# A routed FFN block: gathered rows transposed by the DMA engines in place of TensorE

## The chip, the cores and the metric

One core of a Trainium2 chip runs the kernel. The metric is device time in microseconds (us) of one execution; the time before the change is the median of three runs.

## The reference

`x` is (4, 512, 512), 2,048 tokens of 512 features. A first part adds to it a 512 x 512 matrix per batch, made from scores of a context, of which each row keeps its largest 153. The second part, in which the change lies, is a mixture of experts on the normalised tokens:

```python
logits = x @ router_w.T
topk_w, topk_idx = jax.lax.top_k(softmax(logits), 2)      # 2 of 8 experts a token
topk_w = topk_w / jnp.sum(topk_w, axis=-1, keepdims=True)
...
out = jax.nn.silu(x @ gw) * (x @ uw) @ dw                 # 512 -> 352 -> 512, for each expert
return (acc + ce[:, None] * out, None)
...
shared = jax.nn.silu(x @ s_gate_w + s_gate_b) * (x @ s_up_w + s_up_b) @ s_down_w + s_down_b   # 512 -> 704 -> 512
return (moe_out + shared)
```

## The kernel before

The kernel computes in float16 pairs: a value is a high half plus a low half, and a product is three matmuls (high x high, high x low, low x high). `xn_dram` holds for each token 1,024 float16, the 512 high halves and then the 512 low halves of its normalised row.

**Stages.** Four batches go through attention, residual, normalisation and the shared expert. The last batch's shared expert overlaps with the routing: VectorE and TensorE sort the 4,096 (token, expert) pairs into blocks of 128 that have one expert each. There are at most 39 blocks (`BLOCKS`); with these inputs 35 are run. `run_blocks` (L1443) writes the first 21 out, loops over the next 12 two at a time and takes the rest behind a test of how many are in use.

**One routed block**, number j, parity p = j mod 2:

- GpSimd, `gather` (L538): copies a column of indices to `gidx` (L539) and starts an indirect DMA (L540) of 128 rows of `xn_dram` into `xg[p]`, which lies in `qT` or `kT`, 256 KB.
- TensorE, `routed_x` (L1001): eight float16 transposes (L1009) of `xg[p]` into PSUM bank 0. VectorE, `routed_x` (L1396), copies the bank to `xT2` (L1401), where a parity has one buffer.
- TensorE, `routed_up` (L1012): 24 matmuls of 352 columns (L1023 to L1028), with `xT2` as stationary operand and the expert's gate and up weights moving. Where they lie comes from `where(j)`, a register load from `wbase`.
- ScalarE, `routed_sig` (L785): the Silu of the gate. VectorE, `routed_hidden` (L1407): times the up part.
- TensorE, `routed_hT` (L1031): three float32 transposes (L1036) of the hidden rows to bank 1. ScalarE, `routed_h` (L791), writes the high half and VectorE, `routed_h` (L1412), the low half.
- TensorE, `routed_down` (L1039): nine matmuls of 512 columns (L1047 to L1049).
- ScalarE, `routed_y` (L799): times the token's weight, into `y2[p]`, when the scatter that last used the buffer (j - 2) has landed.
- GpSimd, `scatter` (L543): waits for `y2` and for the landing of the scatter before (tokens can be in both), copies the indices to `sidx` (L551) and starts an indirect DMA (L552) that adds the 128 rows to the output in DRAM.

**Order on each engine**, fixed by `step(j)`. TensorE: hidden transposes of j-1, eight row transposes of j+1, up of j, down of j-1. ScalarE: `routed_h(j-1)`, in the first 21 blocks two conversions of weights (`split_hi`, L600), `routed_sig(j)`, `routed_y(j-1)`. VectorE: `routed_h(j-1)`, `routed_x(j+1)`, in the first 21 blocks two `weight_lo` (L1101), `routed_hidden(j)`. GpSimd: gather(j+3), which waits until the rows of block j+1 have been transposed out of the same buffer, then scatter(j-1). SyncE loads weights through four staging places (L396), each again when VectorE or GpSimd is done with it; the last loads are issued about 480 us into the span.

**Start.** GpSimd gathers blocks 0 and 1, adds three tiles of the shared output, waits for block 0's transposes, gathers block 2 and adds the fourth tile. TensorE transposes the rows of block 0 ahead of the last shared down projection. ScalarE writes four shared outputs (`shared_out`, L693) with weight conversions between them.

Of the kernel before, what the change touches and what calls it, by code (L numbers as in the profile page):

```python
# [5 lines left out]
F32 = mybir.dt.float32  # L6
F16 = mybir.dt.float16
# [6 lines left out]
P = 128  # L14
NB, S, D = 4, 512, 512
# [4 lines left out]
KD = D // P  # L20
# [25 lines left out]
DC, SC = len(DOWN_ROWS), len(SH_ROWS)  # L46
# [9 lines left out]
BLOCKS = T * TOPK // P + E - 1  # L56
# [38 lines left out]
SECOND_AT = [2, 2, 2, 1]  # L95
# [27 lines left out]
def build(nc, x, ctx_in, wq, wk, gamma, router, gate, up, down, s_gate, s_gate_b, s_up, s_up_b, s_down, s_down_b,  # L123
# [3 lines left out]
    def sb(name, shape, dt=F32):  # L127
        return es.enter_context(nc.sbuf_tensor(name, shape, dt))

    def sem(name):  # L130
        return es.enter_context(nc.semaphore(name))
# [22 lines left out]
    xT = sb("xT", [P, 2, KD, S], F16)  # L154
# [6 lines left out]
    ident16 = sb("ident16", [P, P], F16)  # L161
# [37 lines left out]
    xg = [t[:, :].bitcast(F16) for t in (qT, kT)]  # L199
# [3 lines left out]
    y2 = xb[:, 0:2, :]  # L203
    h2 = xb[:, 2:4, 0:I]
    sg2 = sgt[:, :, 0:I]
    xT2 = xT[:, :, :, :].rearrange("p s c t -> p (s c t)")[:, 0:4 * KD * P].rearrange("p (a s c t) -> p a s c t", a=2, s=2, c=KD)
    hT2 = hS[:, :, 0:DC, 0:2 * P].rearrange("p s c (a t) -> p s c a t", a=2)
    rt = sigA[:, :, :].rearrange("p a b -> p (a b)")
# [51 lines left out]
    bank = [es.enter_context(nc.psum_tensor(f"bank{i}", [P, 512], F32)) for i in range(8)]  # L260
# [10 lines left out]
    d_y = [sem(f"d_y{i}") for i in range(2)]  # L271
    d_stage = [sem(f"d_stage{i}") for i in range(PLACES)]
    d_xg = [sem(f"d_xg{i}") for i in range(2)]
    d_sc = [sem(f"d_sc{i}") for i in range(2)]
    s_const = sem("s_const")
    s_zero = sem("s_zero")
# [26 lines left out]
    s_gu = sem("s_gu")  # L303
# [20 lines left out]
    s_oneh = sem("s_oneh")  # L324
    s_tabp = sem("s_tabp")
    s_route = sem("s_route")
    s_x2ps = sem("s_x2ps")
    s_x2 = sem("s_x2")
    s_gu2 = sem("s_gu2")
    s_sig2 = sem("s_sig2")  # L330
    s_h2 = sem("s_h2")
# [6 lines left out]
    s_held = sem("s_held")  # L338
# [100 lines left out]
    def _(pool):  # L439
# [44 lines left out]
        def add_shared(b, t, src):  # L484
            g = TB * b + t
            pool.wait_ge(s_y, g + 1)
            pool.wait_ge(d_x1, 16 * TB * (b + 1))
            pool.dma_start(out[g * P:(g + 1) * P, :], src, accum_op=ALU.add).then_inc(d_y[t % 2], 16)
# [77 lines left out]
        gather(1, 1)  # L566
        for t in range(TB - 1):
            add_shared(NB - 1, t, ylasts[t])
        pool.wait_ge(s_x2ps, 1)
        gather(2, 0)  # L570
        add_shared(NB - 1, TB - 1, ylasts[TB - 1])

        def step(j, m, p, fetch=True):
            if fetch:
                pool.wait_ge(s_x2ps, j + 2)
                gather(j + 3, 1 - p)
            if not (isinstance(j, int) and j == 0):
                scatter(j - 1, m if p else m - 1, 1 - p)
# [10 lines left out]
    def _(act):  # L589
# [12 lines left out]
        def split_some(k):  # L602
            for _ in range(k):
                split_hi(next(loads))
# [88 lines left out]
        def shared_out(b, t, dst):  # L693
            g = TB * b + t
            act.wait_ge(s_yps, g + 1)
            if b < NB - 1 and g >= 2:
                act.wait_ge(d_y[t % 2], 16 * (g // 2))
            act.activation(dst, bank[4 + t][:, :], ACT.Copy, scale=1.0 / HW).then_inc(s_y, 1)
# [75 lines left out]
        act.wait_ge(s_xnT, NT)  # L774
        for i in range(2):
            act.wait_ge(d_xn[i], 16 * NT // 2)
        for t in range(TB):
            shared_out(NB - 1, t, ylasts[t])
            if t == 0:
                split_some(FIRST_AT[SC])  # L780
            split_some(SECOND_AT[t])

        def routed_sig(j, p):
            act.wait_ge(s_gu2, j + 1)
            act.activation(sg2[:, p, :], bank[4 + 2 * p][:, 0:I], ACT.Silu, scale=1.0 / XW).then_inc(s_sig2, 1)  # L785
# [7 lines left out]
        def routed_y(j, m, p):  # L793
            act.wait_ge(s_y2ps, j + 1)
            if isinstance(j, int) and j < 2:
                act.wait_ge(d_y[p], 16 * NT // 2)
            else:
                act.wait_ge(d_sc[p], 16 * m)
            act.activation(y2[:, p, :], bank[2 + p][:, :], ACT.Copy, scale=wcol[:, bass.ds(j, 1)]).then_inc(s_y2, 1)  # L799

        def step(j, m, p, fetch=True):
            first_block = isinstance(j, int) and j == 0
            if not first_block:
                routed_h(j - 1, 1 - p)
            if isinstance(j, int) and j < HEAD_BLOCKS:
                split_some(BLOCK_UNITS)
            routed_sig(j, p)
            if not first_block:
                routed_y(j - 1, m if p else m - 1, 1 - p)

# [2 lines left out]
        def finish(j):  # L813
            routed_h(j, j % 2)
            routed_y(j, j // 2, j % 2)

        run_blocks(act, used, step, finish)

    @block.tensor
    def _(pe):  # L820
# [177 lines left out]
        shared_down(NB - 1, 1)  # L998
        shared_down(NB - 1, 2)

        def routed_x(j, m, p):  # L1001
            pe.wait_ge(d_xg[p], 16 * (m + 1))
            if isinstance(j, int) and j == 0:
                pe.wait_ge(s_route, 1)
            else:
                pe.wait_ge(s_x2, j)
            o = bank[0][:, :].bitcast(F16)
            for c in range(2 * KD):
                last = pe.transpose(o[:, c * P:(c + 1) * P], xg[p][:, c * P:(c + 1) * P], ident16[:, :])  # L1009
            last.then_inc(s_x2ps, 1)  # L1010

        def routed_up(j, p, at):  # L1012
            pe.wait_ge(s_x2, j + 1)
            if not (isinstance(j, int) and j < 2):
                pe.wait_ge(s_h2, j - 1)
            else:
                pe.wait_ge(s_y, NT - 2 + 2 * j)
            og, ou = bank[4 + 2 * p][:, 0:I], bank[5 + 2 * p][:, 0:I]
            for c in range(KD):
                hi, lo = at + (GU_HI + c * GU), at + (GU_LO + c * GU)  # L1020
                xh, xl = xT2[:, p, 0, c, :], xT2[:, p, 1, c, :]
                f, z = c == 0, c == KD - 1
                pe.matmul(og, xh, W[:, bass.ds(hi, I)], start=f, stop=False)  # L1023
                pe.matmul(ou, xh, W[:, bass.ds(hi + I, I)], start=f, stop=False)  # L1024
                pe.matmul(og, xh, W[:, bass.ds(lo, I)], start=False, stop=False)  # L1025
                pe.matmul(ou, xh, W[:, bass.ds(lo + I, I)], start=False, stop=False)  # L1026
                pe.matmul(og, xl, W[:, bass.ds(hi, I)], start=False, stop=z)  # L1027
                last = pe.matmul(ou, xl, W[:, bass.ds(hi + I, I)], start=False, stop=z)  # L1028
            last.then_inc(s_gu2, 1)
# [25 lines left out]
        def step(j, m, p, fetch=True):  # L1055
            first_block = isinstance(j, int) and j == 0
            if not first_block:
                routed_hT(j - 1, 1 - p)
            if first_block or not (isinstance(j, int) and j == BLOCKS - 1):
                routed_x(j + 1, m + (1 if p else 0), 1 - p)  # L1060
            at = where(j)
            if not isinstance(j, int):
                pe.wait_ge(s_wloD, EARLY + (E - 1) * PER_EXPERT)
            elif j == 0:
                pe.wait_ge(s_wlo, SECOND - EARLY)
            elif j % 4 == 0 and j < HEAD_BLOCKS:
                pe.wait_ge(s_wloD, EARLY + j // 4 * PER_EXPERT)
            routed_up(j, p, at)
            if not first_block:
                routed_down(j - 1, 1 - p, where(j - 1))  # L1070

        routed_x(0, 0, 0)
        shared_down(NB - 1, TB - 1)

        def finish(j):
# [6 lines left out]
    def _(dve):  # L1082
# [243 lines left out]
        for k in range(2):  # L1326
            last = dve.tensor_tensor(sel[:, k, :, :], ef[:, k, :].rearrange("p (g o) -> p g o", o=1).to_broadcast([P, NT, E]),
                                     io8.rearrange("p (o e) -> p o e", o=1).to_broadcast([P, NT, E]), ALU.is_equal)
# [20 lines left out]
        for k in range(2):  # L1349
            last = dve.tensor_tensor(prod[:, k, :, :], sel[:, k, :, :], slotr, ALU.mult)  # L1350
# [42 lines left out]
        dve.tensor_scalar(wcol[:, :], tab[:, 1, :], 1.0 / HW, None, ALU.mult)  # L1393
        dve.scalar_tensor_tensor(idx[:, :], tab[:, 0, :], -1.0, zer, ALU.add, ALU.add).then_inc(s_route, 1)

        def routed_x(j, p):  # L1396

            dve.wait_ge(s_x2ps, j + 1)
            if not (isinstance(j, int) and j < 2):
                dve.wait_ge(s_gu2, j - 1)  # L1400
            dve.tensor_copy(xT2[:, p, :, :, :].rearrange("p s c t -> p (s c t)").bitcast(F32), bank[0][:, :]).then_inc(s_x2, 1)  # L1401

        def routed_hidden(j, p):
            dve.wait_ge(s_sig2, j + 1)
            if not (isinstance(j, int) and j < 2):
# [9 lines left out]
        def step(j, m, p, fetch=True):  # L1415
            first_block = isinstance(j, int) and j == 0
            if not first_block:
                routed_h(j - 1, 1 - p)
            if first_block or not (isinstance(j, int) and j == BLOCKS - 1):
                routed_x(j + 1, 1 - p)  # L1420
            if isinstance(j, int) and j < HEAD_BLOCKS:
                later_weights(BLOCK_UNITS)
            routed_hidden(j, p)
# [3 lines left out]
        def later_weights(k):  # L1427
            for _ in range(k):
                weight_lo(next(later))

        later_weights(4)
        routed_x(0, 0)
        later_weights(sum(SECOND_AT) - 4)

        def finish(j):
            routed_h(j, j % 2)
# [51 lines left out]
```

## Time and profile before

| | us |
|---|---|
| median of three runs | 600.37 (599.4 to 602.25) |
| the profiled execution | 601.87 |
| its span in the profile | 599.7 |
| TensorE busy (PE) | 489.7, 82% |
| VectorE busy (DVE) | 355.1, 59% |
| ScalarE busy (ACT) | 241.0, 40% |
| GpSimd busy (POOL) | 194.9, 32% |
| mean granted TensorE clock | 0.908 of full speed |

The span runs from the first to the last recorded instruction of one execution; the execution's own time has some two microseconds around it. PE is TensorE's matmuls, PEld its weight loads, DVE is VectorE, ACT ScalarE, POOL GpSimd and SPq SyncE's queue of DMA issues. A matmul's busy time includes its pipeline, so that TensorE can look busy while it could take more. "idle before" names what the engine was last waiting for.

### The profile page before, as it was taken

The page shows a single profiled execution, that of the slowest core. Times are in us where ns is not written, and L with a number is a line of the kernel's source. Part 1 is how long each engine was busy: PE and PEld are TensorE (multiplying, and loading weights), DVE is VectorE, ACT ScalarE, POOL GpSimd, SP SyncE. Part 2 cuts the span into 40 slices and gives each one's busy share as a digit, 9 for nine tenths or more (in the row PEclk, how much of TensorE's full clock was granted, in tenths as well). Part 3 has the DMA queues.
Part 4 walks back from the last instruction along what each step waited for, and adds up shares of the span by engine and source line. Part 5 has one row for each costly group of instructions (what it writes and reads, how often), then busy time and mean ns, then how long its engine had stood idle before and what let it go on. Part 6 is the DMA issues. An engine that isn't in the chain of part 4 may idle for free.

```text
span 599.7 us, 9826 instructions
## 1 busy us (share of the span) xinstructions
PE 489.7 (82%) x2994; PEld 273.9 (46%) x2995; DVE 355.1 (59%) x987; ACT 241.0 (40%) x433; POOL 194.9 (32%) x245
## 2 busy tenths in 40 slices
PE   6120439959899598968899999999999999999970
PEld 2000324414444154434445555666666666666640
DVE  2799787688586886878269745454554542322210
ACT  4643265353735337451634243443534432222220
POOL 1031243001500033000606743445445454454531
PEclk9565769979899699997999999999999999999985
DMA  6601240003710037001622386777887745445451
GB/s 173 205 18 35 89 147 12 1 1 84 196 21 1 1 107 176 0 0 72 135 79 66 109 230 169 205 178 179 175 200 189 169 87 87 89 80 95 71 91 17
DMA packets 36415, 60.51 MB, mean 101 GB/s; under 512 B 5641, under 2 KB 16137, under 8 KB 36370
## 3 DMA queue, kind: packets, MB, share of 16 engines
q0 software_dynamic: 10384, 23.34, 22.6%
q1 hardware_dynamic: 25986, 36.60, 19.3%
q8 instruction: 25, 0.41, 0.3%
q14 instruction: 20, 0.16, 0.1%
HBM read 37.64 MB, written 22.28 MB: 100 GB/s over the span
## 4 chain that ended last, share of the span: by engine, by line
PE 66%; DVE 20%; issue 5%; ACT 5%; POOL 2%; DMA 1%; DVEq 0%; SPq 0%; POOLq 0%; ACTq 0%
PE bank L912 5%; PE bank L913 5%; PE bank L914 5%; PE bank L1047 4%; PE bank L1049 4%; PE bank L1048 4%; PE bank L1023 3%; PE bank L1025 3%; PE bank L1026 3%; PE bank L1028 3%; PE bank L1027 3%; PE bank L1024 3%; PE bank L927 3%; PE bank L1009 3%; PE bank L929 3%
## 5 line engine op out<-in xcount | busy, mean ns | idle before, releaser
L912 PE MATMUL bank<-xT,W 128*128 128x512 f16 x192 | 74.0, 385 | 0.0
L913 PE MATMUL bank<-xT,W 128*128 128x512 f16 x192 | 73.9, 385 | 0.0
L914 PE MATMUL bank<-xT,W 128*128 128x512 f16 x192 | 73.8, 384 | 0.0
L552 POOL DMA_INDIRECT out_dram<-xb,sidx x35 | 57.0, 1627 | 30.1 <-POOL sidx L551 27.8
L1412 DVE TENSOR_TENSOR hS<-bank,hS 128x384 f16<-128x384 f32 x35 | 19.5, 558 | 73.7 <-ACT hS L791 69.6
L785 ACT ACTIVATE sgt<-bank 128x352 f32<-128x352 f32 x35 | 16.2, 463 | 86.6 <-PE bank L1028 86.6
L1407 DVE SCALAR_TENSOR_TENSOR xb<-bank,sgt 128x352 f32<-128x352 f32 x35 | 18.3, 524 | 54.0 <-ACT sgt L785 53.4
L799 ACT ACTIVATE xb<-bank,wcol 128x512 f32<-128x512 f32 x35 | 24.0, 687 | 56.8 <-PE bank L1049 52.3
L482 POOL TENSOR_TENSOR rstd<-pw 128x4 f32<-128x4 f32 x12 | 13.0, 1087 | 103.7 <-DVE pw L1129 103.7
L1023 PE MATMUL bank<-W,xT 128*128 x140 | 43.8, 313 | 0.6 <-issue 0.5
L1025 PE MATMUL bank<-W,xT 128*128 x140 | 43.8, 313 | 0.0
L1024 PE MATMUL bank<-W,xT 128*128 x140 | 43.8, 313 | 0.0
L1026 PE MATMUL bank<-W,xT 128*128 x140 | 43.8, 313 | 0.0
L1027 PE MATMUL bank<-W,xT 128*128 x140 | 43.8, 313 | 0.0
L1028 PE MATMUL bank<-W,xT 128*128 x140 | 43.8, 312 | 0.0
L652 ACT ACTIVATE sgt<-bank,bias 128x512 f32<-128x512 f32 x24 | 16.5, 687 | 66.9 <-PE bank L914 66.9
L1047 PE MATMUL bank<-W,hS 128*128 x105 | 40.5, 386 | 1.3 <-DVE hS L1412 1.3
L1048 PE MATMUL bank<-W,hS 128*128 x105 | 40.6, 386 | 0.0
L1049 PE MATMUL bank<-W,hS 128*128 x105 | 40.6, 386 | 0.0
L927 PE MATMUL bank<-W,hS 128*128 128x512 f16 x96 | 39.1, 407 | 0.0
L928 PE MATMUL bank<-W,hS 128*128 128x512 f16 x96 | 38.7, 403 | 0.0
L929 PE MATMUL bank<-W,hS 128*128 128x512 f16 x96 | 38.6, 402 | 0.0
(232 smaller groups left out, 1114.9 us busy)
## 6 DMA issues: line engine op xcount, KB each, us to landing
xn_dram<-xn SPq DMA_DIRECT2D x17, 256.0 KB, 2.4
xb<-x_in SPq DMA_DIRECT2D x4, 1024.0 KB, 6.4
out_dram<-xb SPq DMA_DIRECT2D x16, 256.0 KB, 2.1
out_dram<-ysh POOLq DMA_DIRECT2D x12, 256.0 KB, 5.1
stage<-L_ffn_down_w_in SPq DMA_DIRECT2D x12, 256.0 KB
sim<-L_ffn_down_w_in SPq DMA_DIRECT2D x12, 256.0 KB
stage<-L_ffn_gate_w_in SPq DMA_DIRECT2D x16, 176.0 KB
stage<-L_ffn_up_w_in SPq DMA_DIRECT2D x16, 176.0 KB
```

The lines of the kernel that those rows point to most:

```text
L912: pe.matmul(o, wh, xT[:, 0, c, :], start=(c == 0), stop=False)
L913: pe.matmul(o, wh, xT[:, 1, c, :], start=False, stop=False)
L914: last = pe.matmul(o, wl, xT[:, 0, c, :], start=False, stop=(c == KD - 1))
L1023: pe.matmul(og, xh, W[:, bass.ds(hi, I)], start=f, stop=False)
L1024: pe.matmul(ou, xh, W[:, bass.ds(hi + I, I)], start=f, stop=False)
L1025: pe.matmul(og, xh, W[:, bass.ds(lo, I)], start=False, stop=False)
L1026: pe.matmul(ou, xh, W[:, bass.ds(lo + I, I)], start=False, stop=False)
L1027: pe.matmul(og, xl, W[:, bass.ds(hi, I)], start=False, stop=z)
L1028: last = pe.matmul(ou, xl, W[:, bass.ds(hi + I, I)], start=False, stop=z)
L1047: pe.matmul(o, hh, wh, start=(c == 0), stop=False)
L1048: pe.matmul(o, hh, wl, start=False, stop=False)
L1049: last = pe.matmul(o, hl, wh, start=False, stop=(c == DC - 1))
```

## The change

The eight transposes of a block on TensorE, PSUM bank 0's part in them and VectorE's copy go. In their place ScalarE issues one transposing DMA a block (`dma_start_transpose`) from `xg[p]` in SBUF to `xT2[p]` in SBUF, 128 rows x 1,024 float16. It waits for the gather of its block. For blocks 0 and 1 it is issued among the last shared outputs, after the shared outputs of tiles 1 and 2 and the two weight conversions behind each; for block j+2 it is issued in ScalarE's `step(j)` between `routed_sig(j)` and `routed_y(j-1)`. `routed_up` waits on the DMA's semaphore. GpSimd's gathers wait on it too, where they waited for TensorE's transposes. The order of the other work is the same.

```diff
+    xt2 = xT[:, :, :, :].rearrange("p s c t -> p (s c t)")[:, 0:4 * KD * P].rearrange("p (a n t) -> p a n t", a=2, n=2 * KD)
...
+    d_xt = [sem(f"d_xt{i}") for i in range(2)]
...
-        pool.wait_ge(s_x2ps, 1)
+        pool.wait_ge(d_xt[0], 16)
         gather(2, 0)
...
             if fetch:
-                pool.wait_ge(s_x2ps, j + 2)
+                pool.wait_ge(d_xt[1 - p], 16 * (m + 1 + p))
                 gather(j + 3, 1 - p)
...
+        def routed_x(m, p):
+            act.wait_ge(d_xg[p], 16 * (m + 1))
+            act.sem_inc(s_held, 1)
+            act.dma_start_transpose(xt2[:, p, :, :], xg[p][:, :]).then_inc(d_xt[p], 16)
+
         for t in range(TB):
             shared_out(NB - 1, t, ylasts[t])
             if t == 0:
                 split_some(FIRST_AT[SC])
             split_some(SECOND_AT[t])
+            if t in (1, 2):
+                act.wait_ge(s_gu, NB * SC)
+                routed_x(0, t - 1)
...
             routed_sig(j, p)
+            if not (isinstance(j, int) and j + 2 >= BLOCKS):
+                routed_x(m + 1, p)
             if not first_block:
                 routed_y(j - 1, m if p else m - 1, 1 - p)
...
         def finish(j):
             routed_h(j, j % 2)
             routed_y(j, j // 2, j % 2)
+            for i in range(2):
+                act.wait_ge(d_xt[i], 16 * ((min(j + 2, BLOCKS - 1) + 2 - i) // 2))
...
-        def routed_x(j, m, p):
-            pe.wait_ge(d_xg[p], 16 * (m + 1))
+        def routed_up(j, m, p, at):
+            pe.wait_ge(d_xt[p], 16 * (m + 1))
             if isinstance(j, int) and j == 0:
                 pe.wait_ge(s_route, 1)
-            else:
-                pe.wait_ge(s_x2, j)
-            o = bank[0][:, :].bitcast(F16)
-            for c in range(2 * KD):
-                last = pe.transpose(o[:, c * P:(c + 1) * P], xg[p][:, c * P:(c + 1) * P], ident16[:, :])
-            last.then_inc(s_x2ps, 1)
-
-        def routed_up(j, p, at):
-            pe.wait_ge(s_x2, j + 1)
...
-            if first_block or not (isinstance(j, int) and j == BLOCKS - 1):
-                routed_x(j + 1, m + (1 if p else 0), 1 - p)
             at = where(j)
...
-        routed_x(0, 0, 0)
         shared_down(NB - 1, TB - 1)
...
-        def routed_x(j, p):
-
-            dve.wait_ge(s_x2ps, j + 1)
-            if not (isinstance(j, int) and j < 2):
-                dve.wait_ge(s_gu2, j - 1)
-            dve.tensor_copy(xT2[:, p, :, :, :].rearrange("p s c t -> p (s c t)").bitcast(F32), bank[0][:, :]).then_inc(s_x2, 1)
...
-        later_weights(4)
-        routed_x(0, 0)
-        later_weights(sum(SECOND_AT) - 4)
+        later_weights(sum(SECOND_AT))
```

## Rows read from the trace of the kernel before

**Rows 1.** The page's first line.

```profile
span 599.7 us, 9826 instructions
```

**Rows 2.** Stages, cut at scatters 0, 20 and 34 (x: instructions).

```profile
core 0: us, PE busy (x) PEld busy (x) DVE busy (x) ACT busy (x) POOL busy (x), PEclk, DMA share, GB/s
371.48:499.43 127.95, 127.95 (x896) 82.06 (x894) 63.81 (x111) 52.65 (x97) 63.24 (x80) 1.00 0.74 168
499.43:587.94 88.51, 82.75 (x552) 50.96 (x550) 21.24 (x38) 20.80 (x40) 40.73 (x55) 0.96 0.47 81
```

**Rows 3.** TensorE's timeline, one block, and a gap (start, duration, what).

```profile
444.93 0.49 PE L1036 MATMUL bank<-ident,xb 128*128 128x128 f32 x3
445.26 0.61 PE L1009 MATMUL bank<-ident,kT 128*128 128x128 f16 x8
445.70 0.31 PE L1023 MATMUL bank<-W,xT 128*128 x1
...
452.00 0.31 PE L1023 MATMUL bank<-W,xT 128*128 x1
...
503.01 0.32 PE L1023 MATMUL bank<-W,xT 128*128 x1 [0.48 <-issue]
```

**Rows 4.** GpSimd's timeline: scatters 3, 4, 9, 10, a cycle from scatter 21, scatter 25.

```profile
390.70 2.29 POOL L552 DMA_INDIRECT out_dram<-xb,sidx  x1 [0.84 <-POOL sidx L551]
...
399.09 1.61 POOL L552 DMA_INDIRECT out_dram<-xb,sidx  x1 [0.84 <-POOL sidx L551]
...
431.68 1.60 POOL L552 DMA_INDIRECT out_dram<-xb,sidx  x1 [0.84 <-POOL sidx L551]
...
437.59 1.61 POOL L552 DMA_INDIRECT out_dram<-xb,sidx  x1 [0.84 <-POOL sidx L551]
...
505.61 1.60 POOL L552 DMA_INDIRECT out_dram<-xb,sidx  x1 [0.84 <-POOL sidx L551]
506.65 0.77 POOL L539 COPY gidx<-idx 128x1 int32 x1
508.20 1.00 POOL L540 DMA_INDIRECT qT<-xn_dram,gidx  x1 [0.79 <-POOL gidx L539]
510.76 0.18 POOL L551 COPY sidx<-idx 128x1 int32 x1 [1.56 <-DMA out_dram<-xb,sidx]
511.80 1.61 POOL L552 DMA_INDIRECT out_dram<-xb,sidx  x1 [0.85 <-POOL sidx L551]
...
530.11 1.60 POOL L552 DMA_INDIRECT out_dram<-xb,sidx  x1 [0.84 <-POOL sidx L551]
```

**Rows 5.** GpSimd's waits, 371 to 531 us (total, times, longest).

```profile
POOL sidx L551 <- DMA out_dram<-xb,sidx: 38.6, 24, 3.0
...
POOL sidx L551 <- ACT xb L799: 0.9, 1, 0.9
```

**Rows 6.** Short stretches, columns as in rows 2.

```profile
396.00:398.00 2.00, 2.00 (x15) 1.30 (x14) 2.00 (x4) 0.86 (x2) 0.05 (x1) 1.00 0.94 328
...
574.00:575.00 1.00, 1.00 (x9) 0.64 (x8) 0.11 (x1) 0.00 (x0) 1.00 (x2) 1.00 0.00 0
```

**Rows 7.** Timeline of VectorE and TensorE where the routed stage starts.

```profile
359.99 0.61 DVE L1401 COPY xT<-bank 128x512 f32<-128x512 f32 x1
...
362.69 0.55 PE L1036 MATMUL bank<-ident,xb 128*128 128x128 f32 x3 [1.24 <-DVE xb L1407]
363.08 0.61 PE L1009 MATMUL bank<-ident,qT 128*128 128x128 f16 x8
```

**Rows 8.** SyncE's queue: one of its issues of a weight load.

```profile
391.69 0.34 SPq L396 DMA_DIRECT2D stage<-L_ffn_gate_w_in  x1
```

**Rows 9.** The page's DMA issues: count, KB each, us to landing.

```profile
out_dram<-xb SPq DMA_DIRECT2D x16, 256.0 KB, 2.1
...
kT<-ctx_in SPq DMA_DIRECT2D x4, 256.0 KB, 5.4
```

**Rows 10.** DMA queues, 400 to 480 us: packets, MB, share of 16 engines.

```profile
q0 software_dynamic: 2845, 6.61, 47.2%
q1 hardware_dynamic: 5505, 7.87, 33.3%
```

**Rows 11.** DMA queues, 500 to 530 us.

```profile
q0 software_dynamic: 1124, 2.63, 51.6%
```

**Rows 12.** Timeline of the last block: TensorE, and the last scatter.

```profile
580.32 0.52 PE L1036 MATMUL bank<-ident,xb 128*128 128x128 f32 x3 [2.21 <-issue]
...
582.10 0.60 PE L1047 MATMUL bank<-W,hS 128*128 x1 [1.26 <-DVE hS L1412]
582.50 0.63 PE L1048 MATMUL bank<-W,hS 128*128 x1
...
587.94 1.59 POOL L552 DMA_INDIRECT out_dram<-xb,sidx  x1 [0.85 <-POOL sidx L551]
```

More of the change, by code:

```diff
@@ L326, in build @@
     s_route = sem("s_route")
-    s_x2ps = sem("s_x2ps")
-    s_x2 = sem("s_x2")
     s_gu2 = sem("s_gu2")
@@ L1067, in step @@
                 pe.wait_ge(s_wloD, EARLY + j // 4 * PER_EXPERT)
-            routed_up(j, p, at)
+            routed_up(j, m, p, at)
             if not first_block:
                 routed_down(j - 1, 1 - p, where(j - 1))
-        routed_x(0, 0, 0)
         shared_down(NB - 1, TB - 1)
@@ L1418, in step @@
                 routed_h(j - 1, 1 - p)
-            if first_block or not (isinstance(j, int) and j == BLOCKS - 1):
-                routed_x(j + 1, 1 - p)
             if isinstance(j, int) and j < HEAD_BLOCKS:
```

## The prediction

> **What bounds the kernel now.** I read the stages first, then one block on TensorE, then GpSimd's queue, and last the DMA engines.
>
> The scatters of the routed stage run from 371.48 to 587.94 us of a span of 599.7 us [rows 1, 12]. The stage table is cut at scatters 0, 20 and 34: 127.95 us for 20 blocks with weight loads beside them (6.40 us a block), then 88.51 us for 14 blocks (6.32 us) without them. TensorE is busy in every microsecond of the first part [rows 2]. Its timeline shows the block's make-up: from one block's first up matmul (445.70) to the next one's (452.00) are 6.30 us, of which the three transposes of the hidden rows take 0.33 (444.93 to 445.26) and the eight transposes of the gathered rows 0.44 (445.26 to 445.70) [rows 3]. So TensorE looks like the bound, and the eight transposes a part of it.
>
> GpSimd's rows show a second chain that is as long. A scatter may start only when the one before has landed. In the cycle shown, the scatter starts at 505.61, the copy of the next indices starts at 510.76 once it has landed, 5.15 us later, and the next scatter at 511.80: 6.19 us [rows 4]. The gather lies in between and costs the chain nothing. From 371 to 531 us this engine waited 24 times for the scatter's landing before it could copy indices, against one wait for ScalarE in the same stretch [rows 5]. The cycle without loads is (530.11 - 505.61) / 4 = 6.12 us. With loads it is longer, once 8.39 us (390.70 to 399.09) [rows 4], where the DMA engines were 94% busy [rows 6]. That TensorE doesn't wait today is due to the two buffers of `y2`: from scatter 3 (390.70) to scatter 9 (431.68) pass 41.0 us against 6 x 6.30 on TensorE, so the scatters fall 3 us behind, and catch up later. Two bounds lie side by side then: TensorE at 6.30 us and the scatters at 6.12 us without loads, 6.40 us on average with them.
>
> **The change part by part.** One block costs this.
>
> TensorE loses 8 transposes, 0.44 us a block, and comes to 5.85 us. There are 36 such groups, so alone that would be 16 us. The register load of `where(j)` had them ahead of it; what stays ahead is down matmuls and the hidden rows' transposes, longer work than those, so I cost it at 0; if the cover is gone, the one gap of this kind is 0.48 us, before 503.01 [rows 3], and it would eat the whole saving.
>
> VectorE loses one PSUM copy a block (0.61 us for the one at 359.99 [rows 7]) and isn't on the path in the steady state: 63.81 us busy in 127.95 [rows 2].
>
> ScalarE gains one wait, for the gather of block j+2, and one DMA issue, both after `routed_sig(j)`. Queued behind them are `routed_y(j-1)`, `routed_h(j)` and two weight splits. The hold of the issue has no row: from below 0.33 us (an issue on SyncE's queue [rows 8]), from above 1.60 us (GpSimd's indirect one [rows 4]). I take 1.0, between the two. ScalarE is busy 52.65 us in 20 blocks [rows 2], 2.6 of 6.4 a block; of the 3.8 us left I count 2.5 as usable for a hold, since its pieces wait for other engines in between. The wait is harmless for the same reason: the gather starts at 508.20, right behind a scatter, so it has been on its way for most of a cycle by the time the next scatter starts, and what waits for ScalarE, the copy of the indices for `y2`, has some 3 us to spare once the scatters set the pace (a `y2` is written when the scatter before last has landed). `h(j)` is needed only when up(j+1) has run, 3.6 us after the hidden rows' transposes.
>
> The result's landing: 2.1 us for a plain 256 KB transfer at best, 5.4 at worst [rows 9]. It is needed two blocks less one up stage later, 2 x 5.85 - 3.6 = 8.1 us after up(j) ends. Hidden at both ends.
>
> GpSimd's gather(j+3) waits for the transposing DMA of j+1 in place of TensorE's transposes. That DMA is issued a block earlier, ahead of the `y2` of j-2 whose scatter GpSimd issues before this gather, so 0; behind the wait stands scatter(j-1), which a DMA of over about 5 us would begin to delay. SyncE's queue isn't touched.
>
> The 16 DMA engines get the work: 256 KB more a block. At the loads' rate (7.87 MB in 33.3% of 80 us, 3.4 us a MB) that is 0.89 us of all engines [rows 10]. Today they are busy 47.2 + 33.3% with loads, 5.2 of 6.40 us [rows 10], and 51.6% without, 3.2 of 6.12 us [rows 11]. So 2.9 us are free without loads and 1.2 with them. Bounds of what the scatter feels: 0 (all of it falls in the gap, as the empty microsecond after a gather shows [rows 6]) and 0.89 (all of it beside the scatter, as in the collision at 390 to 399 us, where the loads of two units, about 2 us, cost the cycle 2.3). On average the loads' 2.1 us a block cost the scatter 6.40 - 6.12 = 0.28, 13% of their time. With a gap of 1.2 us that share must grow; I take a quarter, 0.22 us, with loads, and 13%, 0.12 us, without.
>
> For the price in engine time the Trainium skill ("Advanced Engine Details and Errata", X-Bar Transpose) says that on trn2 transposing DMAs are as fast as regular ones. By that rule 0.89 stands. No run so far shows one.
>
> Start: the chain to block 1 runs through VectorE's copy at 359.99 and then the transposes of block 0's hidden rows at 362.69 and block 2's gathered rows behind them [rows 7]. Both copies go: 0.54 + 0.45 = -1.0 us. Block 0's and 1's transposing DMAs are issued behind shared outputs and land before 357 us, when the last shared matmul ends.
>
> End: the last block's tail (hidden rows at 580.32, down matmuls from 582.10 [rows 12], last scatter 587.94) takes 9.8 us from the end of the matmuls before it (580.32 - 2.21 = 578.11) and stays; TensorE is over 3 us ahead of the scatters by then, so scatter 34 follows scatter 33, not its tail.
>
> **The sum.** The profiled execution took 601.87 us (span 599.7 and 2.2 around it); the median of the runs is 1.5 lower. With TensorE at 5.85 the scatters set the pace throughout. Start -1.0; 20 blocks with loads x 0.22 = +4.4; 14 blocks x (6.12 + 0.12) = 87.4 against 88.5, -1.1. Together +2.3: 604.2, and 602.7 as a median. The expected 16 us are gone because the scatters, not TensorE, hold the stage.
>
> **The rivals.**
>
> Hidden: the DMA fits into the gaps. Start -1.0, loads 0, then 14 x 6.12 = 85.7 against 88.5, -2.8: -3.8, 596.6. For it: the engines' free time, and that the issue waits for the gather's landing, so it tends to fall right behind it. Against: only 1.2 us are free with loads.
>
> TensorE's saving shows in full: the scatters' cycle would have to close at 5.85, so 34 x 5.85 = 198.9 against 216.5, and -1.0: about 582. Against: the shortest cycle that I found is 5.91 us (431.68 to 437.59 [rows 4]), and the mean without loads 6.12.
>
> Slower, by contention: the transposing DMA's packets lie between the scatter's on the same engines, each block. It decides from 34 x d > 3.8 + 3, d = 0.2 us a scatter. With half of 0.89 (0.45): 20 x 0.45 + 14 x 6.57 - 88.5 - 1.0 = +11.5, 612; with all of it +26.5, 627. For it: 81% busy engines with loads, the collision row. Against: 13% so far.
>
> Much slower, by small pieces: if each row goes in pieces of 128 elements, 1,024 of them, at what a packet of the loads costs (5,505 in 33.3% of 80 us on 16 engines, 77 ns [rows 10]), that is 4.9 us of all engines a block: 10.1 in place of 6.40 with loads and 8.1 in place of 6.32 without, +74 + 25, about 700. For it: nothing in the trace. Against: shorter pieces should cost less than these 1.4 KB ones. Beside it stands a rule that speaks against the change: the Trainium skill ("VectorE: DVE Perf Modes", The three transpose paths) gives 1309 ns for a 128x128 transpose by DMA against 390 ns on TensorE; an estimate from that is 10.5 us for eight, if they go one by one, and the stage would take over 350 us. The row disagrees on TensorE already: eight take 0.44 us.
>
> **How the numbers follow.** About 0.5%, 3 us, is what a measurement can tell. The forecast (598 to 606) has 0.43, of it 0.33 within 0.5% and 0.10 above. Hidden 0.18 and TensorE in full 0.04 are faster, 0.22. Contention 0.25 and small pieces 0.10 are slower, with the forecast's upper part 0.45. The range 595.5 to 622 leaves out TensorE in full, small pieces and the worst of the contention.
>
> **What would show it.** Right: scatter starts 6.2 us apart after 500 us and 6.6 before, GpSimd's waits before the indices still on the DMA, TensorE with gaps before L1047 of some 0.3 us a block, full granted clock, scatter landing above 4.9 us where transposing packets lie beside it. Hidden: the same with 6.1. Small pieces: waits of ScalarE or TensorE on the transposing DMA itself, DMA share at 0.9 in all slices. Wrong altogether: scatter cycles under 6.0, or a granted clock that falls in the gaps as it does after the 2.2 us wait at the end, where a matmul takes 0.63 us [rows 12].

## The result and the profile after

The changed kernel takes 623.31 us (median of 4 runs, 620.64 to 625.85) against 600.85 us of the kernel before beside it: a ratio of 1.035 [1.031, 1.040]. It is slower by 3.5%. At the time first shown that is 600.37 x 1.035 = 621.5 us: just inside the range, far from the forecast's 602.7, and between the two ends of the contention rival, 612 and 627. The profiled execution took 620.64 us, with a span of 618.7. The ratios here and below leave out disturbed executions, of which one program, a_nosc, had two in four.

The stages, cut at scatters 0, 20 and 34 as in [rows 2]:

```profile
core 0: us, PE busy (x) PEld busy (x) DVE busy (x) ACT busy (x) POOL busy (x), PEclk, DMA share, GB/s
369.83:513.34 143.51, 125.72 (x736) 73.00 (x734) 51.27 (x90) 52.09 (x97) 63.05 (x80) 0.99 0.95 187
513.34:607.03 93.69, 78.13 (x448) 44.75 (x445) 13.37 (x25) 20.05 (x39) 40.83 (x54) 0.96 0.66 113
```

Three terms make the difference of the last scatter (607.03 against 587.94, +19.1): scatter 0 comes 1.65 us earlier, the 20 blocks with weight loads take 143.51 against 127.95 (+15.6), the other 14 take 93.69 against 88.51 (+5.2). TensorE, never idle before in the first part, is busy 125.72 of 143.51 us. The DMA engines' share is 0.95 where it was 0.74, and 0.66 where it was 0.47.

GpSimd's timeline, two cycles without loads (compare [rows 4]):

```profile
539.87 1.61 POOL L552 DMA_INDIRECT out_dram<-xb,sidx  x1 [0.85 <-POOL sidx L551]
...
545.66 0.19 POOL L551 COPY sidx<-idx 128x1 int32 x1 [2.19 <-DMA out_dram<-xb,sidx]
546.69 1.60 POOL L552 DMA_INDIRECT out_dram<-xb,sidx  x1 [0.84 <-POOL sidx L551]
...
553.29 1.61 POOL L552 DMA_INDIRECT out_dram<-xb,sidx  x1 [0.85 <-POOL sidx L551]
```

From a scatter's start to the copy that waits for its landing pass 5.79 us, 5.15 before. The cycle is 6.82 and 6.60 us here, and (600.99 - 513.34) / 13 = 6.74 on average up to scatter 33. GpSimd's and ScalarE's waits in the whole routed stage, and TensorE's gap in one block:

```profile
POOL sidx L551 <- DMA out_dram<-xb,sidx: 72.6, 34, 5.6
```

```profile
ACT xb L807 <- issue: 127.8, 29, 7.0
```

```profile
543.28 0.39 PE L1050 MATMUL bank<-W,hS 128*128 x1 [0.36 <-DVE hS L1405]
```

All 34 copies of indices behind the first scatter now wait for a scatter's landing; in the kernel before 25 copies did, and the other 10 waited for ScalarE. GpSimd waits for scatters to land, ScalarE's `routed_y` waits with it, and TensorE's gap before the down matmuls is where that shows. The profile names no releaser for ScalarE's wait, which is what its word "issue" says.

There is a second kind of wait. Who waited for the transposing DMAs themselves (total, times), and the longest of these waits, at the start:

```profile
  POOL gidx L539: 12.5, 6
  PE bank L1026: 7.7, 6
```

```profile
366.74 0.19 POOL L539 COPY gidx<-idx 128x1 int32<-128x1 int32 x1 [6.95 <-DMA xT<-qT]
```

GpSimd's gather waits for the landing six times and TensorE's up matmuls six times, all of it before scatter 20.

What the transposing DMAs themselves cost: the page's queue line, the queues from 520 to 560 us (6 transposing DMAs by their packets), the same from 400 to 480 us (11 of them; compare [rows 10, 11]), and how long an issue holds ScalarE's queue (least, median, most in ns):

```profile
q10 hardware_dynamic: 39072, 9.70, 10.7%
```

```profile
q0 software_dynamic: 1344, 3.15, 45.9%
q10 hardware_dynamic: 6336, 1.57, 20.7%
```

```profile
q0 software_dynamic: 2464, 5.77, 41.1%
q1 hardware_dynamic: 4785, 6.72, 32.3%
q10 hardware_dynamic: 11616, 2.88, 26.0%
```

```profile
L780 ACTq DMA_TRANSPOSE xT<-qT x19: 1247/1257/1576, 347.0 to 595.7; - x19
```

39,072 packets for 37 DMAs are 1,056 each, about 250 bytes. Without loads one DMA keeps all engines busy for 20.7% x 40 / 6 = 1.38 us, with loads for 26.0% x 80 / 11 = 1.89 us. The three queues with loads add up to 99.4%: there the engines are full. The hold on ScalarE's queue is 1.25 us.

Where these packets lie in a cycle, from the queues in short stretches of the cycle that starts with the scatter at 546.69 (the transposing DMA was issued at 546.63): 547.5 to 548.5, 548.5 to 549.0, 549.0 to 549.5, 549.5 to 550.5.

```profile
q10 hardware_dynamic: 539, 0.14, 69.7%
...
q10 hardware_dynamic: 341, 0.09, 101.6%
...
q0 software_dynamic: 16, 0.03, 95.0%
q10 hardware_dynamic: 176, 0.04, 37.0%
...
q0 software_dynamic: 44, 0.09, 86.7%
```

The transposing packets take most of the engines from 547.5 to 549 us, and the scatter's first packets appear only as they end, 2.5 us after its issue. The same reading in steps of 0.1 us gives 2.4 to 2.9 us for eight scatters from 519 to 567 us, against 1.9 to 2.2 us for six scatters of the kernel before. The coincidence is no chance: ScalarE issues the transposing DMA when the gather has landed, and the gather's packets lie right behind the scatter before, so that it comes out together with the next scatter. For the ten scatters from 526.56 to 587.43 us the two issues are at most 0.3 us apart.

### The profile page after: what moved, and what is told of

It is laid out like the page before. It is cut to its first block, busy times and chain, and to the rows that moved or that the text cites. A ratio compares the mean times of both kernels' runs of the same rounds, so it can differ in the third digit from the quotient of the medians.

```text
span 618.7 us, 9238 instructions
## 1 busy us (share of the span) xinstructions
PE 481.8 (78%) x2706; PEld 257.8 (42%) x2707; DVE 333.6 (54%) x951; ACT 239.7 (39%) x433; POOL 195.3 (32%) x245
## 3 DMA queue, kind: packets, MB, share of 16 engines
q1 hardware_dynamic: 25986, 36.60, 19.1%
q10 hardware_dynamic: 39072, 9.70, 10.7%
## 4 chain that ended last, share of the span: by engine, by line
DMA 34%; PE 29%; DVE 18%; issue 9%; ACT 4%; POOL 3%; POOLq 0%; DVEq 0%; SPq 0%; ACTq 0%
DMA out_dram<-xb,sidx 30%; PE bank L924 5%; PE bank L926 5%; PE bank L925 5%; PE bank L939 3%; PE bank L940 3%; PE bank L941 3%; PE bank L870 2%; DVE hS L1281 2%; DVE stats L1124 2%; DVE top L1203 1%; POOL sidx L551 1%; DVE sgt L1290 1%; DMA xT<-qT 1%; DVE W L1370 1%
## 5 line engine op out<-in xcount | busy, mean ns | idle before, releaser
L1050 PE MATMUL bank<-W,hS 128*128 x105 | 40.9, 390 | 14.6 <-DVE hS L1405 13.2
L1052 PE MATMUL bank<-W,hS 128*128 x105 | 41.1, 391 | 0.0
L1051 PE MATMUL bank<-W,hS 128*128 x105 | 41.0, 390 | 0.0
L684 ACT ACTIVATE signs<-sim,nprobe 128x512 int8<-128x512 f32 x40 | 28.4, 714 | 16.6 <-DVE probe L1167 8.6
L503 POOL PARTITION_ALL_REDUCE bad<-bad x4 | 1.5, 383 | 104.7 <-DVE bad L1188 104.7
```

## The experiments

Each is timed beside the kernel before on the same chip. Several leave out a part of the work; the expectation says which. "Cycle" is worked out from the starts of the scatters in each profile: with loads, scatter 0 to 20, divided by 20; without, scatter 20 to 33, divided by 13.

| kernel | us | ratio to before | cycle with loads | without |
|---|---|---|---|---|
| before | 600.9 to 602.9 | | 6.40 | 6.19 |
| changed | 623.3 | 1.035 [1.031, 1.040] | 7.18 | 6.74 |
| a_none | 593.1 | 0.987 [0.982, 0.992] | 6.31 | 5.98 |
| a_plain | 606.1 | 1.006 [1.003, 1.009] | 6.56 | 6.16 |
| a_half | 611.1 | 1.016 [1.011, 1.021] | 6.75 | 6.38 |
| b_extra | 627.7 | 1.046 [1.037, 1.055] | 7.18 | 6.81 |
| a_noload | 614.5 | 1.022 [1.018, 1.026] | 6.78 | 6.71 |
| b_early | 601.5 | 1.000 [0.998, 1.003] | 6.40 | 6.27 |
| a_early | 622.3 | 1.030 [1.021, 1.039] | 6.92 | 6.54 |
| a_move | 616.4 | 1.020 [1.016, 1.024] | 6.87 | 6.77 |
| a_move_early | 611.4 | 1.017 [1.012, 1.022] | 6.82 | 6.22 |
| a_none_early | 589.7 | 0.979 [0.976, 0.982] | 6.06 | 5.88 |
| b_nosc | 590.9 | 0.982 [0.977, 0.986] | | |
| a_nosc | 586.4 | 0.967 [0.959, 0.975] | | |

The theory that I began with was the rival of contention: the transposing packets delay the scatters, whose cycle bounds the stage. Its own rival was ScalarE's queue: in-order waits and the hold make `y2` late.

**a_none: the DMA away, the waits kept.**

```diff
-            act.dma_start_transpose(xt2[:, p, :, :], xg[p][:, :]).then_inc(d_xt[p], 16)
+            act.sem_inc(d_xt[p], 16)
```

> The changed kernel without the transposing DMAs: ScalarE still waits for the gather at the same places and TensorE multiplies whatever lies in xT2 (the routed part of the output is not computed from its rows). Contention theory (the transposing packets share the DMA engines with the scatter): scatter cycle back to 6.1 us without loads and 6.3 to 6.4 with them, against 6.7 and 7.2, total 595 to 599 us. Queue theory (ScalarE's in-order wait for the gather makes y2 late): the wait is still there, so 612 to 623 us. If the scatters did not bound the stage at all, TensorE's 5.85 us a block would give about 583 us.

It took 593.1 us, 2 us below the expected range, since the cycle without loads came down to 5.98 us and not 6.1. That is what the scatters' chain takes when nothing else is on the engines but gathers: the 6.19 us before the change were partly waits for `y2`. The 6.12 us that the prediction used, where nearly all waits were for a landing, is still 0.14 above it, and why isn't shown. ScalarE waits for the gather at the same places, so that wait costs nothing that shows; what the change loses, it loses with the DMA. The scatter's packets come 2.1 us after its issue again. This run doesn't test the waits for the DMA's landing, which are met at once here.

**b_extra: the DMA alone, added to the kernel before.**

```diff
...
+            act.wait_ge(d_xg[p], 16 * (m + 1))
+            act.sem_inc(s_held, 1)
+            act.dma_start_transpose(xt3[:, p, :, :], xg[p][:, :]).then_inc(d_xt[p], 16)
...
```

Nobody reads `xt3`. GpSimd's gathers wait for this DMA too.

> The kernel before, with its transposes on TensorE, plus the changed kernel's transposing DMAs at the same places in ScalarE's queue into a part of xT that nobody reads. Contention theory: all of the loss without any of the rest of the change, scatter cycle 6.7 us without loads, 7.1 with them, 620 to 627 us. If the loss came from the removed parts or from TensorE waiting for rows that land late: 600 to 604 us.

627.7 us, at the upper end of the range, with the changed kernel's cycles (7.18 and 6.81). All of the loss comes with the added DMA and none with what was taken away. The 4 us above the changed kernel lie at the start: in this profile scatter 0 comes at 377.61 us, behind a weight load that took 10.02 us to land. TensorE doesn't wait for the DMA here and the cycles are the same, so its waits in the changed kernel add nothing to them; what GpSimd's waits add with loads is not separated.

**b_early and a_early: 1.0 us out of the scatters' cycle.**

```diff
             if not (isinstance(j, int) and j == 0):
+                pass
+            link2(pool.tensor_copy(sidx[:, p:p + 1], idx[:, bass.ds(j, 1)]), s_si, j + 1)
+            if not (isinstance(j, int) and j == 0):
                 pool.wait_ge(d_sc[1 - p], 16 * (m + 1) if p else 16 * m)
-            link2(pool.tensor_copy(sidx[:, p:p + 1], idx[:, bass.ds(j, 1)]), s_si, j + 1)
+                pool.sem_inc(s_held, 1)
```

> The kernel before with the copy of a scatter's indices moved ahead of the wait for the landing of the scatter before, which takes about 1.0 us (0.18 of copy and 0.84 behind it) out of the scatters' cycle. TensorE at 6.30 us is the bound then as it nearly is now: 598 to 601 us. If the scatters held the kernel before back as well, 592 to 597.

601.5 us, no difference to the kernel before, as expected: before the change TensorE sets the pace at 6.30 us, and the scatters keep up. The cycle with loads stays at 6.40 us with 1.0 us taken out of the scatters' chain, so the chain alone did not set it.

> The changed kernel with the same move of the index copy. Contention theory with the scatters' cycle as the bound: cycle 6.7 - 1.0 = 5.7 us without loads, where TensorE's 5.85 takes over, and 7.2 - 1.0 = 6.2 with them: 588 to 596 us, a gain over both kernels. Queue theory (ScalarE's wait for the gather or the transposing DMA's hold is the bound): 615 to 623 us, nearly nothing gained.

622.3 us: missed by far, and informative. The cycle fell by 0.2 us, not 1.0. GpSimd's timeline shows the scatter issued at 543.52 and the next only at 550.24:

```profile
543.52 1.61 POOL L555 DMA_INDIRECT out_dram<-xb,sidx  x1 [2.47 <-DMA out_dram<-xb,sidx]
...
550.24 1.60 POOL L555 DMA_INDIRECT out_dram<-xb,sidx  x1 [2.92 <-DMA out_dram<-xb,sidx]
```

Its packets came in strength only from 547.0 us, 3.5 us after the issue (2.0 in the kernel before), because the transposing packets lay at 545.0 to 547.5 us: the gather's landing (issue at 544.16) still fixed them. An earlier scatter only waits longer for the engines; the next one, issued nearly together with its transposing DMA, had its packets after 2.6 us. That suggests one series on the DMA engines: scatter's data, gather's data, landing and issue, transposing data, the next scatter's data. Over the routed stage the shorter cycles still save 8 us. They went at the start, where one weight load beside the first transposing DMAs took 11.55 us to land, and scatter 0 came at 379.46 instead of 369.83. In the chain that ended last:

```profile
355.25 11.55 DMA sim<-L_ffn_up_w_in
```

That gave a new theory, "serial", against plain contention by engine time.

**a_half: the DMA of the high halves only.**

```diff
-            act.dma_start_transpose(xt2[:, p, :, :], xg[p][:, :])
+            act.dma_start_transpose(xt2[:, p, 0:KD, :], xg[p][:, 0:KD * P])
```

> The changed kernel with the transposing DMA of the high halves only (512 of the 1,024 columns; the low halves in xT2 are stale, so the routed output is not computed in full). Serial theory, new after the first runs (each cycle goes one after the other through scatter data, gather data, the gather's landing at ScalarE, the transposing data, and only then the next scatter's data): half of 1.5 us of transposing data gone from every cycle, 6.0 to 6.1 us without loads, total 603 to 609. A fixed cost per DMA, whatever its size: 615 to 622.

611.1 us, somewhat above the serial theory's range and below the fixed price's. The cycle without loads is 6.38 us where the serial theory had 6.0 to 6.1, so that theory is right in direction and too strong in size. Against a_none's cycle the half costs 0.40 us and the whole 0.76 without loads, 0.44 and 0.87 with them: the price goes by size. It is not the hold of ScalarE's queue, which hardly changed:

```profile
L780 ACTq DMA_TRANSPOSE xT<-qT x19: 1206/1212/2262, 347.1 to 583.5; - x19
```

**a_plain: a plain DMA of the same bytes in its place.**

```diff
-            act.dma_start_transpose(xt2[:, p, :, :], xg[p][:, :]).then_inc(d_xt[p], 16)
+            act.dma_start(xt2[:, p, :, :].rearrange("q n t -> q (n t)"), xg[p][:, :]).then_inc(d_xt[p], 16)
```

> The changed kernel with a plain DMA from xg to xT2 of the same 256 KB in the transposing DMA's place (the rows arrive untransposed, so the routed output is not the reference's). If only bytes count (transposing DMAs cost what regular ones do): 620 to 625 us, as the changed kernel. If the transposing DMA's price is its 1,056 small packets (1.4 to 1.7 us of all engines against some 0.8 at the loads' rate): cycle 6.2 to 6.4 us without loads, total 603 to 612.

606.1 us. Its queue from 520 to 560 us, 7 DMAs of 144 packets:

```profile
q10 hardware_dynamic: 1008, 1.84, 12.4%
```

That is 0.71 us of all engines each, half of the transposing DMA's 1.38, and a quarter of its cost in the cycle (0.18 of 0.76 us), though it is issued as near to the scatter (0.1 to 0.4 us behind it). So engine time alone is not the price either: a_half's 528 packets keep the engines for about 0.65 us, no longer than these 144, and cost twice as much. The costs follow the number of packets (144, 528 and 1,056 for 0.18, 0.40 and 0.76 us), but how fast the issue frees ScalarE changed along with it (0.47 us here), and the two were not varied apart. The Trainium skill's rule that transposing DMAs are as fast as regular ones ("Advanced Engine Details and Errata", X-Bar Transpose) doesn't hold here: from SBUF to SBUF the same 256 KB take twice the engine time.

**a_noload: the weight loads away.**

```diff
-                sp.dma_start(place[:, at:at + cols], src).then_inc(loaded, 16)
+                if n >= SECOND:
+                    sp.sem_inc(loaded, 16)
+                else:
+                    sp.dma_start(place[:, at:at + cols], src).then_inc(loaded, 16)
```

> The changed kernel without the weight loads of all but the first routed expert (stale weights, so the routed output is not the reference's). The DMA engines are full in the stretch with loads (99.9% from 400 to 480 us). If that is why its cycle is 7.18 us and not 6.74: 20 x 0.44 = 9 us less, 611 to 616 us. If the loads have no part in it: 621 to 625.

614.5 us. The first 20 blocks fall from 7.18 to 6.78 us, the value of the other 14 (6.71). The loads cost 0.4 us a block, the rest is there without them. Most of that 0.4 isn't new: without the transposing DMA (a_none) the cycles with and without loads are already 0.33 us apart.

**a_move and a_move_early: another moment for the same DMA.**

```diff
...
                 routed_h(j - 1, 1 - p)
+            if not (isinstance(j, int) and j + 1 >= BLOCKS):
+                routed_x(m + p, 1 - p)
...
             routed_sig(j, p)
-            if not (isinstance(j, int) and j + 2 >= BLOCKS):
-                routed_x(m + 1, p)
...
```

> The changed kernel with the transposing DMA of block j+1 issued after routed_h(j-1) instead of that of block j+2 after routed_sig(j): the same DMAs, the gather landed long before, so that ScalarE and the next scatter no longer wait behind a transposing DMA issued at the gather's landing. Serial theory: the link from gather to scatter is cut, the transposing data lie beside the scatter's second half and the gather's; cycle 6.2 to 6.6 us without loads, 604 to 616 us. Plain contention theory (the engine time alone counts, wherever it is put): 620 to 626 us as the changed kernel.

616.4 us, on the edge, but the cycle without loads did not move (6.77). The trace tells why:

```profile
542.04 1.60 POOL L552 DMA_INDIRECT out_dram<-xb,sidx  x1 [0.84 <-POOL sidx L551]
542.07 1.26 ACTq L780 DMA_TRANSPOSE xT<-kT  x1
```

`routed_y` ahead of it waits for the landing of a scatter, as GpSimd's copy does, and so the two issues come out 0.03 us apart by another road. The place in the code moved, the moment did not.

> The changed kernel with both moves, of the transposing DMA and of the index copy. Serial theory: 1.0 us more off the scatters' cycle than with the first move alone, 5.9 to 6.2 us, 593 to 606 us. Plain contention theory: 620 or more, as the changed kernel with the index copy moved (622.3).

611.4 us, above its range, but without loads the cycle is 6.22 us: the scatter is now issued first (538.15), its packets start at 540.0, 1.9 us later, and the transposing DMA (541.08) comes behind scatter and gather. With the whole transposing DMA in place the cycle is as short as that of the kernel before (6.19). It is not free: with the same early index copy and no transposing DMA the cycle is 5.88 us (a_none_early, below). Of the 0.66 us that it cost in a_early, the other moment gives back 0.32. The single cycles are uneven, 5.54 to 7.78 us, and in the longest the next gather was issued 3 us later than usual, behind the DMA's landing. With loads, where the engines have no gap (a share of 1.00 from 380 to 440 us), the cycle stays at 6.82:

```profile
380.00:440.00 60.00, 54.90 (x329) 32.47 (x328) 24.62 (x41) 25.91 (x46) 28.95 (x36) 1.00 1.00 216
```

So without loads the moment makes about half of the price. With loads another moment hardly helps (6.92 to 6.82 us); that full engines are the reason fits the share of 1.00, but no run shows it by itself.

**a_none_early, b_nosc, a_nosc: what TensorE alone gains.**

> No transposing DMA and the index copy moved: TensorE alone should bound the routed stage at 5.85 us a block (the routed output is not computed from its rows). Both theories: 34 x 5.85 from the first scatter to the last, 586 to 590 us, against 593.1 with the scatters' cycle as the bound. If something else holds 6.0 us a block (ScalarE's wait for the gather), it stays at 592 to 594.

589.7 us, at the upper edge of its range. TensorE's timeline, hidden transposes to hidden transposes of the next block:

```profile
530.39 0.49 PE L1042 MATMUL bank<-ident,xb 128*128 128x128 f32 x3
530.87 0.32 PE L1029 MATMUL bank<-W,xT 128*128 x1
531.03 0.31 PE L1030 MATMUL bank<-W,xT 128*128 x1
...
536.40 0.49 PE L1042 MATMUL bank<-ident,xb 128*128 128x128 f32 x3
```

That is 6.01 us, not 5.85: the first up matmul starts 0.48 us after the hidden transposes, which take 0.33. But this block is one of the twelve that run in the loop. In the blocks that are written out, the same two kinds of matmul follow each other without such a loss:

```profile
386.35 0.49 PE L1042 MATMUL bank<-ident,xb 128*128 128x128 f32 x3
386.67 0.31 PE L1029 MATMUL bank<-W,xT 128*128 x1
...
392.19 0.49 PE L1042 MATMUL bank<-ident,xb 128*128 128x128 f32 x3
```

There the block takes 5.84 us, as the prediction had it. The kernel before takes 6.30 us in either kind of block, so in the loop the eight transposes had covered 0.16 us. What it is in the loop, the register load of `where(j)` or something else, is open.

> The kernel before without its 35 scatters (the routed part is computed and not added to the output). TensorE bounds it: the blocks stay at 6.30 us, only the last scatter's landing goes, 592 to 597 us. If the scatters held it, more than 8 us less than before.

```diff
-            pool.indirect_dma_start(out=out, out_offset=bass.IndirectOffsetOnAxis(ap=sidx[:, p:p + 1], axis=0),
-                                    in_=y2[:, p, :], in_offset=None, compute_op=ALU.add).then_inc(d_sc[p], 16)
+            pool.sem_inc(d_sc[p], 16)
```

590.9 us, 11 below before, more than expected and past the mark set for "the scatters held it", but not from the blocks: they stay at 6.30 us, as in the kernel before except for two blocks near 500 us (6.94 and 6.45). So the scatters hardly slowed them. The last block's hidden transposes come 2.3 us earlier (578.02 for 580.32), and the rest is the last scatter and its landing.

> The changed kernel without its scatters. If all that the transposing DMA costs goes through the scatters' cycle: TensorE at 5.85 us a block, 14 to 17 us less than the kernel before without scatters, 576 to 582 us. If the transposing DMA also makes TensorE or ScalarE late by itself (1.25 us of hold, rows that land late): 586 us or more.

586.4 us, the median of four (578.8 to 588.9), above the expected 576 to 582. By the ratios, 0.982 and 0.967, the gain over b_nosc is 9 us, where 14 to 17 were expected; the far ends of the two intervals allow 1 to 16. The twelve blocks of the loop explain 12 x 0.16 = 2 us of the difference; the rest stays open. Without scatters the change pays, then, and with them it does not.

## Why the prediction was right and wrong

Right was the frame. TensorE and the scatters were two bounds side by side, the 16 us of saved transposes could not appear, and the outcome hung on what the new packets do to the scatters. ScalarE's wait for the gather costs nothing by itself (a_none), the hold was 1.25 us for 1.0 predicted, the start gave 1.65 us for 1.0 predicted, and small pieces came as the trace didn't show them: 1,056 packets a block, but at about 21 ns each, not 77, and eight transposes in one DMA took 1.38 us, not the 10.5 of eight in a row.

Wrong was the choice of the likeliest case: "contention", given 0.25, is what happened. That the time lies inside the range is luck: its upper end of 622 was drawn to leave out only the worst of that rival, the sum gave 602.7, and the signs named for a right forecast, scatters 6.2 and 6.6 us apart, did not come (6.74 and 7.18). Two terms of the sum failed.

The price in engine time, "0.89 us of all engines": 1.38 us without loads and 1.89 with them. Bytes were the wrong measure; a_plain, the same bytes without transposing, takes 0.71.

The share that falls on the scatter, "a quarter ... with loads, and 13% ... without": against the cycles of today that the prediction used, 6.40 and 6.12, the cycle grew by 0.78 and 0.62 us for 0.22 and 0.12 predicted; against a_none by 0.87 and 0.76, about half of the engine time in both. The 13% was taken from the weight loads, which come at moments of their own. The transposing DMA is issued at the gather's landing, and without loads it met the next scatter within 0.3 us in ten cycles in a row. I even counted the wait for the gather in favour of "hidden" ("so it tends to fall right behind it"), where it was what tied the two together. And 1.2 us free with loads could not take 1.89.

The sum with the measured terms: -1.65 at the start, 20 x (7.18 - 6.40) = 15.6, and 93.7 - 88.5 = 5.2, together 19.1 us in the span, against +2.3 forecast.

Two smaller misses. The landing was put down as "Hidden at both ends" and GpSimd's wait for it costed at 0; in fact TensorE waited for it six times (7.7 us) and GpSimd six times (12.5 us), all before scatter 20, and scatter 0 was issued only behind such a wait. b_extra shows that TensorE's waits added nothing to the cycle. And the cover of the first up matmul, costed at 0, is worth 0.16 us, but only in the twelve blocks of the loop; the 5.85 us are right for the written-out ones. It decided nothing here.

## What to carry to other kernels

Here work that was moved from an engine to the DMA queues cost what its packets and the moment of its issue made it cost, not what its bytes and average shares promised. So price it that way: ask which event releases it and what else that event's chain releases. Where a kernel has a chain of landings (here each scatter waits for the one before), a DMA that is released by the same chain can delay it in each cycle, here also in the stretch where the engines' share is only 0.66. Before taking time from the engine that looks full, measure the second bound by an experiment that removes the new cost and keeps the waits; here it would have shown 593 us as the most that a free transpose brings with the rest of the kernel as it is.

## What the runs showed of the hardware

A transposing DMA of 128 x 1,024 float16 from SBUF to SBUF makes 1,056 packets and keeps the 16 engines busy for 1.38 us, 1.89 beside loads, against 0.71 us for a plain copy of the same bytes. A scatter issued together with it has its first packets 2.4 to 2.9 us after the issue, against 1.9 to 2.2 us in the kernel before. A single weight load beside the first of these DMAs took 11.55 us to land in one profile (a_early) and 10.02 us in another (b_extra). No version with the transposing DMA and the scatters beat the kernel before; one that uses it only in the blocks without loads, or with a third buffer for the gathered rows so that it can be issued a cycle earlier, wasn't tried.
